# Graph network kernel: both edge relations counted in one number, and one-hots made by compares with a per-partition scalar

## The reference

```python
out = x @ W_root + bias
for r in range(2):
    w = (edge_type == r)
    msg = x[src] @ W_rel[r] * w[:, None]
    sums = segment_sum(msg, dst)
    cnt = segment_sum(w, dst)
    out = out + sums / maximum(cnt, 1.0)[:, None]
...
agg = segment_sum(h[src], dst)      # the second network, both relations together
```

## Time and profile before

| | us |
|---|---|
| median of three runs | 587.81 (587.09 to 589.5) |
| the profiled execution's own time | 587.64 |
| its span from the first to the last instruction | 585.8 |
| counting stage, first DVE addition to the last | 24.6 to 167.0 |
| relation stage, about | 167.5 to 265 |

### The profile page before, as it was taken

The page is one execution under the profiler, slowest core; times in us unless marked ns, Lnnn a source line. Parts: engine busy times, 40 slices in busy tenths (PEclk is TensorE's granted clock), DMA queues, the critical chain, the costliest instruction groups (busy, mean ns, idle before and its releaser), DMA issues.

```text
span 585.8 us, 8370 instructions
## 1 busy us (share of the span) xinstructions
PE 570.0 (97%) x2584; PEld 395.6 (68%) x2584; DVE 379.7 (65%) x980; ACT 231.6 (40%) x477; POOL 100.7 (17%) x80
## 2 busy tenths in 40 slices
PE   7999999999999999999999999999999999999992
PEld 3556656665577676775898888877878867455541
DVE  7599888888847888888602330018748667755455
ACT  5444455533224546463421221013223134276555
POOL 3000000000000000003165512402202230132230
PEclk8999999999999999999999999999999999999997
DMA  9510011111031121128300000700100100021123
GB/s 270 145 35 10 27 36 35 35 35 35 0 92 37 35 72 37 38 76 237 129 27 0 0 0 1 223 4 1 38 0 0 36 1 0 2 70 49 58 70 105
DMA packets 20870, 30.73 MB, mean 52 GB/s; under 512 B 5428, under 2 KB 15254, under 8 KB 20838
## 3 DMA queue, kind: packets, MB, share of 16 engines
q1 hardware_dynamic: 20422, 29.66, 17.2%
q10 hardware_dynamic: 416, 0.67, 0.4%
HBM read 25.20 MB, written 5.12 MB: 52 GB/s over the span
## 4 chain that ended last, share of the span: by engine, by line
PE 94%; DMA 2%; DVE 2%; ACT 1%; POOL 0%; SPq 0%; issue 0%
PE banks L744 20%; PE banks L943 12%; PE banks L1029 12%; PE banks L863 12%; PE banks L730 5%; PE banks L833 5%; PE banks L965 4%; PE banks L955 4%; PE banks L892 4%; PE banks L894 4%; PE banks L873 3%; PE banks L1019 3%; PE banks L837 2%; PE banks L848 1%; PE banks L738 1%; DMA cb_b<-in_L_gnn_conv_bias 1%
## 5 line engine op out<-in xcount | busy, mean ns | idle before, releaser
L744 PE MATMUL banks<-w_all,xnT 128*125 128x429 f32 x320 | 130.4, 532 | 1.9 <-DMA w_all<-in_L_gnn_W_rel 1.9
L744 PEld LDWEIGHTS banks<-w_all,xnT 128*125 128x125 f32 x320 | 54.6, 190 | 32.1 <-issue 29.7
L1192 DVE TENSOR_TENSOR adj<-adj,banks 125x220 f32 x160 | 60.8, 380 | 19.5 <-PE banks L730 17.4
L863 PE MATMUL banks<-hT,w_s 128*128 128x250 f32 x320 | 68.7, 375 | 0.1
L863 PEld LDWEIGHTS banks<-hT,w_s 128*128 128x128 f32 x320 | 60.2, 189 | 8.8 <-issue 1.9
L892 PE MATMUL banks<-y_hi,adj 125*125 125x288 f32 x200 | 55.2, 304 | 0.2 <-issue 0.2
L894 PE MATMUL banks<-y_lo,adj 125*125 125x286 f32 x200 | 53.5, 294 | 0.0
L730 PEld LDWEIGHTS banks<-oh_code,oh_low 125*128 125x128 bf16 x320 | 31.0, 97 | 32.0 <-issue 27.9
L1174 DVE TENSOR_TENSOR oh_code<-iota_c,edge 125x880 bf16<-125x880 f16 x80 | 48.7, 609 | 0.0
L1336 DVE TENSOR_SCALAR hT<-banks,g_c,b_c 128x125 f32<-128x125 f32 x60 | 19.4, 400 | 45.1 <-PE banks L848 45.0
L943 PE MATMUL banks<-adj,h_hi 125*128 125x250 f32 (+1 forms) x180 | 48.2, 367 | 0.0
(11 more groups left out here) (206 smaller groups left out, 884.4 us busy)
## 6 DMA issues: line engine op xcount, KB each, us to landing
xt<-in_x SPq DMA_DIRECT2D x15, 448.0 KB
out_x<-ot SPq DMA_DIRECT2D x9, 448.0 KB
w_s<-in_L_gnn_W SPq DMA_DIRECT2D x5, 512.0 KB, 6.0
xn<-in_x SPq DMA_DIRECT2D x5, 448.0 KB
wd_s<-in_L_gnn_Wd SPq DMA_DIRECT2D x1, 2048.0 KB, 13.7
w_all<-in_L_gnn_W_rel SPq DMA_DIRECT2D x6, 286.0 KB, 6.8
wo_s<-in_L_gnn_wo_weight SPq DMA_DIRECT2D x1, 1024.0 KB, 6.5
w_all<-in_L_gnn_W_root SPq DMA_DIRECT2D x3, 286.0 KB, 6.4
```

Of the source, the lines that this page charges most:

```text
L744: ins = pe.matmul(pb[0:P, 2 + 2 * v + n, 0:FH], xnT[:, u], w_all[:, u, n * FH:(n + 1) * FH], start=(u == 0), stop=(u == KD - 1))
L863: ins = pe.matmul(pb[:, 4 + f % 2, 0:2 * P], w1_s[:, k, f * 128:(f + 1) * 128], hT[:, k], start=(k == 0), stop=(k == KD - 1))
L1192: dve.tensor_tensor(cols, cols, window(b, q), ALU.add).then_inc(done, 1)
```

## The change

Counts of relation 0 and relation 1 go into one number: an edge of relation 0 counts 1, one of relation 1 counts 4096 (`BIG`). The matrix `cnt` is [125, 10, 1274], at the place of `adj`'s relation 0, and a window has 110 numbers, no longer 220.

- DVE: `codes` becomes four `tensor_scalar` instructions of 110 elements, each comparing a line of window positions with a per-partition scalar (`farC`) and multiplying by another (`value`, 1 or 4096). `place` adds 110 elements. The start of the program has some more small instructions.
- PE: `count` has 110 columns; four more small turnings at the start (`e_mark`).
- ScalarE: `filled` goes over `cnt` alone (three fills, before six and a first one), and a new `split(k)` runs for each 250 destinations that are complete: `near = cnt + 1.5 * 2**35` rounds to multiples of 4096, then `adj[:, 1] = near - 1.5 * 2**35`, two instructions of 2500 elements a partition.
- GpSimd: a new `part(k)` makes `adj[:, 0] = cnt - adj[:, 1]`, 2500 elements a partition, five times.
- The sum of relations takes relation 1 times 1/4096, and the counts are compared with 1 and 4096.
- The test that the edges lie well enough is changed to match; the other path (`far_counted`) stays for edges that don't.

```diff
-SPAN = 16
+SPAN = 8
+BIG = 4096.0
+ROUND2 = 1.5 * 2 ** 35
+DONE = 2 * P
...
+            def part(k):
+
+                cols = slice(k * DONE, (k + 1) * DONE)
+                pool.wait_ge(high_set, k + 1)
+                pool.tensor_tensor(adj[:, 0, :, cols], cnt[:, :, cols], adj[:, 1, :, cols], ALU.subtract).then_inc(parted, 1)
+
             for t in range(T):
                 pool.wait_ge(y_copied, 1 + t + 1)
                 pool.tensor_tensor(y_lo[:, t], y_f[:, t], y_hi[:, t, 2:2 + 2 * F], ALU.subtract).then_inc(y_split, 1)
+                if t in (3, 5, 7, 8):
+                    part((3, 5, 7, 8).index(t))
+            part(T // 2 - 1)
...
+            def split(k):
+
+                cols = bass.ds(k * DONE, DONE)
+                act.wait_ge(counts_free, k * (2 * UG) + 2 * UG + 2)
+                act.activation(near[:, :, cols], cnt[:, :, cols], ACT.Identity, bias=up[:, 0:1]).then_inc(near_set, 1)
+                act.wait_ge(near_set, k + 1)
+                act.activation(adj[:, 1, :, cols], near[:, :, cols], ACT.Identity, bias=down[:, 0:1]).then_inc(high_set, 1)
...
                 if cleared is not None:
-                    filled(1 - v, bass.ds(cleared, CS), CS).then_inc(adj_rest, 1)
+                    filled(bass.ds(cleared, CS), CS).then_inc(adj_rest, 1)
+                if complete is not None:
+                    split(complete)
                 evacuate(t, v)
...
-            tile_of_1(T - 1, 1, None, True)
+            tile_of_1(T - 3, 1, 32 * (T // 2 - 1) + 32, False)
+            tile_of_1(T - 2, 0, 32 * (T // 2 - 1) + 32, False, None, T // 2 - 3)
+            tile_of_1(T - 1, 1, None, True, None, T // 2 - 2)
+            act.wait_ge(counts_free, G + 2)
+            split_last()
...
             def count(b):
+
+                for q in range(H):
+                    for j in range(JH):
+                        ins = pe.matmul(pb[:, b, q * C:(q + 1) * C], oh_low[:, b, q, :, j],
+                                        oh_both[:, b, q, j], start=(j == 0), stop=(j == JH - 1))
+                return ins
...
                     if t >= 2:
                         pe.wait_ge(pre_elu, t - 1)
+                    if t % 2 == 0:
+                        pe.wait_ge(parted, t // 2 + 1)
...
+            def codes(g, b):
+
+                for q in range(H):
+                    for j in range(JH):
+                        k = q * JH + j
+                        ins = dve.tensor_scalar(oh_both[:, b, q, j], iota_m[:], one(farC, g, k), one(value, g, k),
+                                                ALU.is_equal, ALU.mult)
+                return ins
...
                 if placed:
-                    cols = adj[:, :, :, bass.ds(base[q], W)]
+                    cols = cnt[:, :, bass.ds(base[q], W)]
                     dve.tensor_tensor(cols, cols, window(b, q), ALU.add).then_inc(done, 1)
...
                 cols = slice(t * P, (t + 1) * P)
-                dve.tensor_tensor(adj[:, 0, :, cols], adj[:, 0, :, cols], adj[:, 1, :, cols], ALU.add).then_inc(adj_sum, 1)
+                dve.scalar_tensor_tensor(adj[:, 0, :, cols], adj[:, 1, :, cols], 1.0 / BIG, adj[:, 0, :, cols], ALU.mult,
+                                         ALU.add).then_inc(adj_sum, 1)
```

More of the change, by code:

```diff
@@ L457, in evacuate, with split_last, tile_of_1 @@
                 act.activation(whole[:, FA:2 * F], pb[0:P, 3 + 2 * v, 0:FH], ACT.Copy, scale=rstd).then_inc(y_copied, 1)
-            def tile_of_1(t, v, uses, last, cleared=None):
+            def split_last():
+                cols = slice(N - DONE, N)
+                act.activation(near[:, :, cols], cnt[:, :, cols], ACT.Identity, bias=up[:, 0:1]).then_inc(near_set, 1)
+                act.wait_ge(near_set, T // 2)
+                act.activation(adj[:, 1, :, cols], near[:, :, cols], ACT.Identity, bias=down[:, 0:1]).then_inc(high_set, 1)
+            def tile_of_1(t, v, uses, last, cleared=None, complete=None):
                 act.wait_ge(xnT_ps, t * 2 + 2)
@@ L906, in _ @@
                     pe.wait_ge(s_onehots, i + 1)
-                    count(0).then_inc(s_counts_mm, 1)
+                    far_count(0).then_inc(s_counts_mm, 1)
                 pe.wait_ge(adj_done, 1)
@@ L1120, in _ @@
             dve.wait_ge(typ_in, 16)
-            step(dve.scalar_tensor_tensor(e_mark[:], typ_i[:], 0.5, e_blk[:], ALU.mult, ALU.add))
+            dve.tensor_scalar(e_mark[:], typ_i[:], BIG - 1.0, 1.0, ALU.mult, ALU.add)
             for q in range(H):
                 part = slice(q * JH * P, (q + 1) * JH * P)
-                ins = dve.scalar_tensor_tensor(e_code[:, part], dst_i[:, part], bounds[:, q:q + 1], e_mark[:, part],
+                ins = dve.scalar_tensor_tensor(e_code[:, part], dst_i[:, part], bounds[:, q:q + 1], e_blk[:, part],
                                                ALU.subtract, ALU.add)
@@ L1147, in _ @@
             dve.scalar_tensor_tensor(gaps[0:1, NG:NG + NS], ends[0:1, 0, SPAN:NG], -float(W), ends[0:1, 0, 0:NS], ALU.add, ALU.subtract)
+            dve.scalar_tensor_tensor(gaps[0:1, 2 * NG + NS + 3:2 * NG + NS + 7], iota_r[0:1, 5:21:5], -50.0,
+                                     ends[0:1, 0, 4 * UG:16 * UG + 1:4 * UG], ALU.mult, ALU.add)
             dve.scalar_tensor_tensor(gaps[0:1, 2 * NG + NS:2 * NG + NS + 3], iota_r[0:1, 7:20:6], 50.0,
@@ L1213, in tile_of_1 @@
                     if more:
-                        codes(g + 2, b, edge[:, 1]).then_inc(onehots, 1)
+                        codes(g + 2, b).then_inc(onehots, 1)
                     if u + 1 < rows:
@@ L1242, in far_counted @@
                         lows(g, 0)
-                        codes(g, 0, codeF).then_inc(s_onehots, 1)
+                        far_codes(g, 0).then_inc(s_onehots, 1)
                         dve.wait_ge(s_counts_mm, w * G - G + g + 1)
@@ L1247, in far_counted @@
                             cols = adj_x[:, :, :, bass.ds(base[q], W)]
-                            dve.tensor_tensor(cols, cols, window(0, q), ALU.add).then_inc(s_added, 1)
+                            dve.tensor_tensor(cols, cols, far_window(0, q), ALU.add).then_inc(s_added, 1)
                             dve.wait_ge(s_added, (w * G - G + g) * H + q + 1)
+                dve.tensor_scalar(adj_x[:, 1], adj_x[:, 1], BIG, None, ALU.mult).then_inc(s_added, 1)
+                dve.wait_ge(s_added, NW * G * H + 1)
             def after_counts():
```

89 lines of the change are left out of this document (55 added, 34 removed).

## The result

The changed kernel takes 628.46 us (median; 626.56 to 629.15) against 587.81 (587.09 to 589.5): 1.0686 times as long, 95% interval 1.0667 to 1.0705. The direction was the forecast one, the size was not: 603 with a range to 616 stood there. The profiled execution took 626.56 us with a span of 624.8, 39.0 more than the 585.8 before.

The account below looks back on a forecast made before the run. PE bounded the old kernel with DVE 12% behind; changed, DVE would bound, held by each `part`. Counting stage 9.6, relations' start 4.1 and clock 1.7 sum to 15.4 us on 587.64: 603 us, range 592 to 616.

Parts of the forecast that it names:

- PE's part: Counting stage on PE: a count falls from 0.40 to 0.24 us, the tile's floor from 16.0 to 14.6.
- The engine time of a group: VectorE's instructions in a counting group: additions 0.185 each, low one-hots 0.333, four codes 0.86 us.
- the weighing's row: Existing instructions with two per-partition scalars, 0.316 us apart; taken to show some 0.06 us a scalar for the new codes.
- Rival 2: Scalars are fetched during the instruction ahead: codes 0.40 us, VectorE group 1.17, PE bounds again, 594 us; chance 10%.
- rival 3: Codes miss four elements a tick (9 us), or each stand costs its clock (5 more): 608 to 614 us; chance 16%.
- The step that failed: VectorE's counting group: codes 0.86 us plus a constant 0.07 for reading the next base, 1.63 us in all.
- GpSimd's part: Each 5.5-us `part` stops VectorE at its next low one-hots: 4.7 us each, four in the counting stage, 18.8 us.
- Rival 1: GpSimd lets VectorE in between rows of a long instruction, so `part` costs nothing: 578 us, faster; chance 16%.
- VectorE's path: Counting stage: start, 78 groups, reciprocals, `y_lo` and `part` put the last addition's end at 176.6 us for 167.0, +9.6.
- The start of the relations: VectorE's sum of the relations waits for the last `part`, with the elu's tails behind it: +4.1 us on PE.
- The clock behind it: PE's clock falls to half after its stands, in the counting stage and at the elu: taken as 1.7 us.
- the step that decides: Whether GpSimd's `part` holds VectorE for the whole instruction; above about 1.5 us a hold, the kernel gets slower.

Follow-up runs that it names:

- a_late_two: a_late with the codes in two instructions of 440 elements and the register load issued ahead of the second addition; 579.17 us, 0.9867 of the kernel before.
- a_late: Changed kernel, VectorE's counting-stage program written out, subtractions on VectorE, the four late ones two relation tiles ahead of their reader; 583.94 us, 0.9947 of the kernel before.
- a_unroll: Changed kernel with VectorE's counting-stage program written out, so scalars stand at constant addresses; subtractions stay on GpSimd; 613.76 us.
- a_early: Changed kernel with the register load for the next group's columns moved ahead of the second addition, behind the low one-hots; 623.95 us.
- a_best_two: Changed kernel, VectorE's program written out, subtractions on VectorE (late ones one relation tile ahead), codes in two instructions of 440 elements; 627.62 us.
- a_fixed: Changed kernel with the four scalar compares of a group reading code and value from a fixed column, so no computed addresses; 614.36 us.
- a_pieces: Changed kernel with each of GpSimd's five subtractions cut into ten of 25 destinations; 617.75 us.

## Why the prediction was right in direction and wrong in size

- **PE's part** held as a whole. With VectorE out of the way a tile takes 14.7 us (forecast floor 14.6). That it is so near is in part luck: a count takes 0.21 us (forecast 0.24, bounds 0.20 and 0.40), but a step of products went from 1.45 to 1.50 us (a_late_two, 71.25 to 72.75), for which the forecast had no term. The estimate of 0.32 for four pairs, from TensorE: Matmul & The Clock Gate of the Trainium skill, section Back-to-back issue gap, does not agree with the 0.21; the measurement decides.
- **The engine time of a group** held, nearly to the hundredth. Additions 0.18 (0.185), low one-hots 0.34 (0.333), codes 0.22 apart (0.215): 1.57 us together, as the runs without computed addresses show, against 1.56 without the reading of the base. The scalars do cost what the weighing's row suggested. Rival 2 falls, and so does the half of rival 3 that has the codes miss four elements a tick. The estimate of 0.36 us for four codes from the formula in VectorE: DVE Perf Modes of the Trainium skill, section on the errata, does not agree either (0.88 measured).
- **The step that failed** is "the codes 0.60, of which 0.07 is the reading of the next base", carried over as a constant into "2 x 0.185 + 0.333 + 0.86 + 0.07 = 1.63". The 0.07 was not a price but the end of a 0.53-us register load, the rest of which one code instruction covered. What the runs showed in its place is a second path through the group, that of the sequencer: 1.53 us before, 1.87 with the change, beside 1.57 of instructions. Four instructions with computed scalar addresses start the load later; the same term is now 0.31, the group 1.88. Over the 72 looped groups that is 72 x 0.25 = 18.0 us on VectorE's path, less 6 x 0.06 = 0.4 in the ninth tile, which is written out and has groups of 1.57; taking it away gave back 14.1 to 14.7 us of the time in three different ways (13.5 to 14.9 against the kernel before on the same chip), since the tiles with a subtraction win little from it. The rows of the sequencer (528 ns for the load) stood in the trace of before, though not in the timeline that was read.
- **GpSimd's part** held in its mechanism, and its price was too low: a second term that was mis-sized. An instruction takes 5.47 us (5.5), and a group with a subtraction takes 6.78 for 1.88, 4.9 lost (4.7). Rival 1 falls by the 6.17-us row. Three of the four holds met the scalar compares already, the fourth the low one-hots (5.59 us at 188.84). GPSIMD Engine Reference of the Trainium skill, section Specifications, names instructions that use both ports as contended beside those with two SBUF inputs; that these compares use both ports no run shows, that they are held the row does. What "4.7 us each, 18.8 in all" left out is what follows a hold: a tile with one takes 22.9 us for 17.5, 5.4 more, and where VectorE's groups are 1.57 long the four cost 27.1 us (a_late against a_unroll), with `y_lo` behind the subtraction and PE at half clock. So the half of rival 3 that has each stand cost its clock stays, and with the sequencer's part taken away the time is 613.8 and not the 603 of the forecast.
- **VectorE's path** adds up so, against the 176.6 forecast for the last addition: start 23.6 for 25.0, -1.4; the base, +17.6; the holds 4 x 0.2, +0.8; together 193.6. The remaining 6.2 us to the 199.8 measured lie in the first two tiles (18.2 for 17.4 each), in the groups behind a hold and in the last tile. VectorE's waits for PE after its first addition, 6.6 us in all, are about as much, and the forecast's path had none. That last attribution is argued from the waits, no run isolates it.
- **The start of the relations** held in size (+4.5 for 4.1), by another instruction than forecast. The sum of the relations was to wait for the subtraction; it was the elu's minimum, ahead of it, that was held (4.34 us for 0.31), and either can go on only when the subtraction ends (213.02). The clock behind it held too (+1.7 for 1.7): it is 0.50 from about 215.5 to 219.
- The sign did not hang on the step that failed: without the sequencer's part the kernel is still 4.4% slower than before (a_unroll), by the hold that the forecast had taken for the step that decides.

## What to carry to other kernels

VectorE had two times for an instruction here: its own, and that of the sequencer ahead of it, which computed addresses and loaded registers one after the other. A row of instructions in which the engine never stands, as the earlier trace rows, does not show which of the two sets the pace. A loop-carried address (0.07 us) is a third of an instruction of 0.2 us, and a register load of 0.5 us needs that much queued work behind the last thing handed over; before splitting one instruction into four, ask what the long one was covering. Work that was moved to GpSimd was paid by VectorE's compares for as long as the instruction lasted: in this kernel VectorE does the same subtraction in half the time for which it would be held (2.75 us for 5.47). A merge that shortens PE's work need not pay: here it did so only once the load, the addresses and the new work were all kept off the path, +6.9% as written and -1.3% with these three moved.

## What the hardware showed unexpectedly

- A register load from SBUF on VectorE's sequencer takes 523 to 558 ns, and nothing behind it is handed over meanwhile: the idle time follows the load wherever it is put (0.21 us ahead of the first addition, 0.24 ahead of the second in a_early, 0.32 with shorter instructions in a_best_two).
- Computing the addresses of an instruction with loop-dependent operands takes that sequencer 46 to 81 ns; each of the codes' addresses comes 0.15 us after the one ahead. Written out in straight code these records are gone for the codes, the low one-hots and the load, and the whole is worth 14.7 us here (the codes' alone 14.1, a_fixed).
- Compares with one SBUF tensor and two per-partition scalars are held by GpSimd's two-input instruction as fully as compares with two SBUF tensors (5523 and 5586 ns at most, for 308 and 419 usual), where the additions with a PSUM operand in the earlier trace rows and in a_pieces (0.25 us inside a piece of 0.73) were not. Pieces of 0.73 us let one compare through at a time.
- Ten pieces of 250 elements take GpSimd 7.24 us in a row and one of 2500 takes 5.46, so cutting in ten makes the sum 33% longer and the kernel 10.7 us faster.
